# Attention and feed-forward in one kernel: upper halves of rows ahead of a step's scores, and the bias of V on ScalarE a step later

## The reference

```python
x = x + _layernorm(_L0_attn_ref(_layernorm(x), Wqkv, bqkv, Wo, bo))
x = x + _layernorm(_L0_ffn_ref(_layernorm(x), gate_w, gate_scale, up_w, up_scale, down_w, down_scale))
```

## Time and profile before

| | |
|---|---|
| median of 3 runs | 1654.09 us (1651.8 to 1659.24) |
| the profiled execution | 1659.15 us, span of the trace 1657.3 us |
| mean granted TensorE clock | 0.975 of full speed |
| TensorE (PE) busy | 1552.0 us, 94% of the span |
| VectorE (DVE) busy | 941.8 us, 57% |
| ScalarE (ACT) busy | 775.8 us, 47% |
| GpSimd (POOL) busy | 644.8 us, 39% |

### The profile page before, as it was taken

How to read it: one execution, slowest core, us unless ns; L and a number is a source line. 1 busy time by engine, 2 the same in 40 slices (tenths; PEclk the granted TensorE clock), 3 DMA queues, 4 the chain that set the end, 5 groups by cost and what they waited for, 6 DMA issues and landing times.

```text
span 1657.3 us, 24457 instructions
## 1 busy us (share of the span) xinstructions
PE 1552.0 (94%) x9288; PEld 641.0 (39%) x9288; DVE 941.8 (57%) x1897; ACT 775.8 (47%) x1252; POOL 644.8 (39%) x844
## 2 busy tenths in 40 slices
PE   4899899988999899999897899999999999999997
PEld 2334234323333333343332244444444444444443
DVE  5657665778656777766777333464434343434344
ACT  5356566557566666755775643233222222222222
POOL 4336675677666677757766520020000000000001
PEclk8899999999999999999998999999999999999999
DMA  4222232213411233321354531221111111111000
GB/s 178 90 52 53 56 73 52 58 53 102 113 49 39 78 90 84 95 54 39 116 159 127 161 96 39 51 93 48 51 26 52 26 51 26 51 26 52 0 26 26
DMA packets 113397, 112.25 MB, mean 68 GB/s; under 512 B 69632, under 2 KB 69632, under 8 KB 113024
## 3 DMA queue, kind: packets, MB, share of 16 engines
q1 hardware_dynamic: 113280, 110.69, 23.5%
HBM read 45.37 MB, written 25.17 MB: 43 GB/s over the span
## 4 chain that ended last, share of the span: by engine, by line
PE 65%; POOL 13%; DVE 10%; ACT 6%; issue 5%; POOLq 0%; ACTq 0%; DVEq 0%
PE ps L966 25%; PE ps L887 13%; PE ps L983 12%; PE ps L950 9%; POOL pt L1452 5%; DVE mcol L1240 4%; PE ps L924 4%; ACT pt L1094 3%; POOL rs L1372 1%; PE ps L900 1%; POOL rec L1462 1%; POOL pt L1443 1%; POOL stage L1436 1%; DVE st L1135 1%; POOL atl L1466 1%
## 5 line engine op out<-in xcount | busy, mean ns | idle before, releaser
L1094 ACT ACTIVATE pt<-ps,nrm 128x512 f32<-128x512 f32 (+1 forms) x640 | 362.4, 645 | 264.6 <-PE ps L924 252.4
L966 PE MATMUL ps<-x2in,gu 128*128 128x512 f16 x2048 | 462.5, 379 | 0.1
L1240 DVE TENSOR_REDUCE mcol<-ps 128x1 f32<-128x512 f32 (+2 forms) x600 | 305.4, 575 | 134.3 <-PE ps L900 67.8
L966 PEld LDWEIGHTS ps<-x2in,gu 128*128 128x128 f16 x2048 | 200.2, 98 | 241.9 <-ACT sg L1115 0.5
L1369 POOL TENSOR_SCALAR rs<-mv 128x1 f32<-128x1 f32 x120 | 24.3, 202 | 655.6 <-DVE mv L1139 649.5
L1311 DVE SCALAR_TENSOR_TENSOR hf<-ps,usc,sg 128x512 f32<-128x512 f32 x128 | 96.1, 751 | 259.2 <-PE ps L966 246.5
L1120 ACT ACTIVATE hh<-hf 128x512 f16<-128x512 f32 x128 | 80.7, 631 | 258.9 <-DVE hf L1311 245.3
L1452 POOL TENSOR_TENSOR pt<-pt 128x1024 f32<-128x1024 f32 x84 | 201.4, 2419 | 0.0
L924 PE MATMUL ps<-qpack,kpack 98*128 98x512 f16 (+3 forms) x768 | 168.1, 335 | 32.5 <-DVE mcol L1240 23.6
L983 PE MATMUL ps<-wd,hh 128*128 128x512 f16 x496 | 188.0, 379 | 0.0
L983 PE MATMUL ps<-wd,hl 128*128 128x512 f16 x496 | 188.0, 379 | 0.0
(11 more groups left out here) (125 smaller groups left out, 1635.8 us busy)
## 6 DMA issues: line engine op xcount, KB each, us to landing
qpack<-stage SPq DMA_DIRECT2D x192, 64.0 KB, 2.0
kpack<-stage SPq DMA_DIRECT2D x192, 64.0 KB, 2.0
xr<-in_x SPq DMA_DIRECT2D x32, 256.0 KB, 2.9
x1d<-xr SPq DMA_DIRECT2D x32, 256.0 KB, 2.3
x2d<-xh SPq DMA_DIRECT2D x32, 256.0 KB, 2.0
x1in<-x1d SPq DMA_DIRECT2D x8, 1024.0 KB, 6.0
out_x<-yy SPq DMA_DIRECT2D x32, 256.0 KB, 2.0
xin<-in_x SPq DMA_DIRECT2D x24, 256.0 KB, 3.1
```

Of the source, the lines that this page charges most:

```text
L966: mm = pe.matmul(bk, GU[:, c, m, i * 128:(i + 1) * 128], x2in[:, 1 - k, p, c, :], start=p == 0 and c == 0, stop=p == 1 and c == 3)
L1094: act.activation(Pt[:, PBUF[step], h, off:512], ps[:, BANK[job], off:512], ACT.Exp, scale=esc).then_inc(s_ex, 1)
L1240: mm = dve.tensor_reduce(mcol[:, n % 2, col:col + 1], scores, AX.X, ALU.max)
```

## The change

Three things are done. The turns of a step move from behind the scores, `invert` and `normalise` to a place ahead of the products and the scores, behind `mjob`. The halving of the divided numerators becomes a job of its own, `halve`, which stands at the same early place one step after the division (step 1 or step 4; at the end of attention for the last one). And the bias of V, which GpSimd added, is added by ScalarE as the first part of `halve`; GpSimd's copy and subtraction follow it by the semaphore s_ab.

```diff
             if of < NG:
                 add(("mjob", of, lot))
+            plan += [job for job in here if job[0] in ("ln1_turn", "turn2")]
+            if (s == 1 and n > 0) or s == 4:
+                add(("halve", n if s == 4 else n - 1, 0 if s == 4 else 1))
             products = products_of(pend, n, s)
...
-            plan += [job for job in here if job[0] in ("ln1_turn", "turn2")]
             plan += [job for job in here if job[0] not in ("ln1_turn", "turn2")]
...
-    plan += [("den",) + pend, ("num",) + pend, ("invert",) + pend[:2], ("normalise",) + pend[:2]]
+    plan += [("den",) + pend, ("num",) + pend, ("invert",) + pend[:2], ("normalise",) + pend[:2], ("halve",) + pend[:2]]
...
+                elif kind == "halve":
+                    n, j = a
+                    e.wait_ge(s_small, SCALED)
+                    e.wait_ge(s_at, NO[job])
+                    act.activation(rec[:], rec[:], ACT.Identity, bias=bvcol[:, n % 4:n % 4 + 1]).then_inc(s_ab, 1)
...
-                elif kind == "normalise":
+                elif kind == "halve":
                     n, j = a
-                    b, g = divmod(n, 4)
                     cols = slice(j * 512, (j + 1) * 512)
                     if n >= 5:
                         e.wait_ge(s_wo, NO["woproj", 8 * ((n - 5) // 4) + 4 * j + 3])
-                    e.wait_ge(s_at, NO[job])
-                    e.wait_ge(s_small, SCALED)
-                    pool.tensor_scalar(rec[:], rec[:], bvcol[:, g:g + 1], None, ALU.add).then_inc(s_ab, 1)
                     e.wait_ge(s_ab, NO[job])
                     pool.tensor_copy(atT[0][:, n % 5, cols], rec[:]).then_inc(s_ah, 1)
```

## The result

The changed kernel takes 1639.01 us (median of 4 runs, 1638.2 to 1639.51) against 1656.25 us of the kernel before on the same chip (4 runs): ratio 0.9894, 95% interval 0.9873 to 0.9916. The profiled execution took 1638.2 us with a span of 1636.3; against the profiled one of before that is 21 us less, all of it in the attention stage.

A forecast was written before the change was run, and what follows sets the result against it. Bound by TensorE in the attention stage, busy 741.28 of 807 us; -15 - 4 - 2 - 10 + 7.8 + 2 + 1.5 = -19.7 us gives 1639 from the profiled 1659.15, 1634 from the median 1654.09; range 1614 to 1656 (8 in 10).

The forecast's parts named there:

- Stalls behind VectorE: Attention stage: nine TensorE stalls behind VectorE's late lower half (L640), sum 18.0 us; turns moved ahead would win 15.
- the lock rival: L640 still falls into GpSimd's sums, nothing won in six n with running sums: -6 us, 1648; chance 0.12.
- Half clock: Eight half-clock stretches after the stalls hold 37.4 us, costing up to 17 us; 10 us would come back.
- Masks of steps 1 and 2: GpSimd, freed of the bias, makes step 1's masks earlier, also in n=14 and 15: sum 5.8 us, 4 taken.
- Step 8: Earlier statistics on VectorE let GpSimd's sums start earlier, shortening TensorE's wait for masks: 2 us won (ends 0 and 8).
- masks at step 8 take it back: Rival: TensorE reaches step 8 earlier and waits for GpSimd; some 10 us given back, -10 in all, 1644; chance 0.12.
- ScalarE's bias: Bias and turn delay step 4's exponentials in 14 n, 7.8 us lost; waits for the division in the last two n, 1.5.
- Transfers: L1013 waits for a transposing transfer's landing in n=5, 6, 9, 10, delaying exponentials: 2 us lost (ends 0 and 6).
- the 51.8 us: VectorE's wait for ScalarE's upper half (L1013) ahead of L640 in the attention stage; sign of right: below 15.
- the 21.4 us: TensorE's wait for VectorE's row maxima (L1240) in the attention stage; sign of right: below 8.
- the 27.0 us: TensorE's wait for GpSimd's masking of the scores (L1443) in the attention stage; sign of right: nearer 20.
- The rival by which ScalarE waits for the division in front of the exponentials: Step 4's margin gone in all 14 n, costing 28 us instead of 7.8: +10, 1664 us; chance 0.12.

## Why the prediction was right, and where its terms were not

The forecast's -19.7 us from the profiled 1659.15 became -20.95 (1638.2); in medians 1634 was forecast and 1639.01 measured. That the turns ahead of the scores make the gain is shown by the run with the turns alone (0.9892) and the one without them (1.0016). Term by term:

- *Stalls behind VectorE, -15 of 18.0.* Measured -13.1: seven of the nine are gone or below 0.9 us, those of n = 5 and 9 stay at 2.04 and 2.03. There the lock rival was right in kind: the sums now hold the residual in front of the eviction.
- *Half clock, -10.* Over all stretches at half clock, not the eight alone that the forecast went by, TensorE's busy time fell from 51.96 to 33.29 us; at the full level that work takes half, so 9.3 us came back. Right; the clock did not come back whole, 34.0 us are left at half.
- *Masks of steps 1 and 2, -4.* TensorE's idle time for them (it falls into steps 2 and 3) went from 16.5 to 12.2 us. Right in size. Its opposite, the price of the new place in GpSimd's queue, I had not seen: I counted the leaving bias, not that copy and subtraction move into the way of the sums.
- *Step 8, -2.* Wrong in sign: 10.6 us became 13.7. That is the rival "masks at step 8 take it back", with 3 us instead of 10. As it said, the sums did not start earlier: in n = 4 the first began 28.1 us behind the group's first matmul before and 29.0 after, while TensorE came to step 8 3.2 us sooner. The reason it gave, halving that begins later, is not the whole: with the turns alone, and the halving at its old place, the first sum began at 28.8 us and the masks of step 8 were waited for 17.5 us.
- *ScalarE's bias, +7.8 and +1.5.* The step that failed is "whatever delays these exponentials reaches TensorE whole". Over n = 1 to 13 it reached step 5 with 4.6 us, not 7.8, and in n = 1, 5 and 9 not at all; of that about 2 us were given back, most of it where TensorE waits for the masks anyway; net about 2.4. The last two groups cost 2.4 instead of 1.5. Together 4.8 for 9.3. The term also took the same activation at 0.65 us in eight n and at 0.74 in six; at 0.65 throughout it would have been 7.4.
- *Transfers, +2.* ScalarE waited 4.8 us for them in four places. What of it reached TensorE was not separated.
- *Not forecast:* n = 0 took 60.81 us for 57.55; as it began 1.0 us earlier, n = 1 began 2.3 us later. GpSimd's sums begin earlier there and hold a split of the output weights on VectorE (2.33 us for 0.86), and a stretch at half clock (120.7 to 124.1 us) follows that the kernel before did not have.

Of the signs named ahead, the 51.8 us (2.6), the 21.4 us (6.8) and the clock came as said; the 27.0 us did not (26.6), and step 5 became longer by the bias in ten of n = 1 to 13, not in each. Of the signs of being wrong two showed: the lower half still takes 2 us or more in n = 1 and 12 (2.84 and 2.33 us; eight such places before), and one wait for exponentials in step 5 is above 1 us (1.72, n = 12). The total came out right partly by luck: the bias was priced 4.5 us too dear, and step 8, n = 0 and the two stalls that stay made up for it. The terms as measured add up to -16.5 us; the other 4.4 us I have not placed. The rival by which ScalarE waits for the division in front of the exponentials stayed small: 6.3 us of waits in four places, all in n = 14 and 15. The 44 turns that the prediction names are VectorE's of the whole kernel; the list has 48 in these groups, which no term hangs on.

## What to carry to other kernels

Moving a job ahead in all queues pays where the engine that ends last waits for it, and costs on every queue where it leaves idle time for busy time: read each engine's idle time in front of the old place and of the new one. When a stall goes, look at what next reads two operands beside the same neighbour, or waits in the same queue; here the collision went from the lower half to the residual, to the split and to a join over 16 columns. Taking away the join's second operand freed the join, and the collision went on to a copy for which TensorE does not wait.

## What the runs showed of the hardware

A VectorE instruction of 16 columns with two operands in SBUF took 2.20 us beside a running sum of GpSimd, and 0.18 us as a reduction with one operand: its size does not protect it. A rounding copy of 32x128 values with one operand, which then stood beside the sums, took 1.03 us in the mean, 0.24 in the changed kernel. GpSimd's addition of a column to 128x512 values took 1.57 us alone, VectorE's 0.49 and ScalarE's 0.71. The three instructions on 128x1 values for a deviation (0.19, 0.55 and 0.27 us) cost GpSimd more than two masks of 128x256 (0.42 each).
